# Second pass of graph attention on one core: the Newton step of a tile moved between the scans and the next tile's rows, ScalarE's norms ahead of its squares

## What is computed

```python
alpha = e_exp / (denom[dst] + 1e-16)          # a softmax over the edges of a dst node, 8 heads
msg = h[src] * alpha[:, :, None]
out = segment_sum(msg, dst)                   # 256 features
x1 = layernorm(x + relu(out + bias))          # eps 1e-5, over the 256 features
```

## Time and profile before

| what | value |
|---|---|
| median of 3 runs | 1858.53 us (1857.64 to 1864.1) |
| profiled execution, its own time | 1859.5 us |
| its span in the profile | 1857.8 us |
| TensorE / VectorE busy | 62% / 68% of the span |
| ScalarE / GpSimd busy | 54% / 54% |
| second pass of attention | from about 540 to 716 us of the span |
| first convolution | from 716.7 us |

### The profile page before, as it was taken

The page is one execution under the profiler, slowest core; times in us unless marked ns, Lnnn a source line. Parts: engine busy times, 40 slices in busy tenths (PEclk is TensorE's granted clock), DMA queues, the critical chain, the costliest instruction groups (busy, mean ns, idle before and its releaser), DMA issues.

```text
span 1857.8 us, 17164 instructions
## 1 busy us (share of the span) xinstructions
PE 1146.6 (62%) x3863; PEld 584.9 (31%) x3863; DVE 1264.9 (68%) x3084; ACT 997.7 (54%) x2650; POOL 998.6 (54%) x1032
## 2 busy tenths in 40 slices
PE   0148888850039972999995999897999891000000
PEld 0023333310014431555552455454444451000000
DVE  8847777769889980555552556464666697778887
ACT  4736877765446772344442465454555454555654
POOL 1057766677777667777763777406444077720000
PEclk9999999975555555999997999998999996555555
DMA  8367899977865653788883566857765288999998
GB/s 360 116 212 233 278 350 375 356 243 230 254 235 174 208 186 112 221 261 266 260 241 113 136 176 178 169 147 128 150 138 128 75 278 327 372 351 350 351 342 315
DMA packets 177393, 436.13 MB, mean 235 GB/s; under 512 B 28804, under 2 KB 108810, under 8 KB 157324
## 3 DMA queue, kind: packets, MB, share of 16 engines
q1 hardware_dynamic: 109020, 229.52, 35.8%
q0 software_dynamic: 44800, 100.49, 21.6%
q10 hardware_dynamic: 23472, 105.03, 15.6%
HBM read 257.16 MB, written 182.32 MB: 237 GB/s over the span
## 4 chain that ended last, share of the span: by engine, by line
PE 30%; DVE 27%; DMA 17%; POOL 11%; issue 8%; ACT 7%; SPq 1%; ACTq 0%; DVEq 0%; POOLq 0%
DMA arena<-x 13%; PE ps L1247 10%; PE ps L1260 10%; POOL arena L1218 4%; DVE arena L1510 3%; DVE arena L1493 3%; PE ps L1237 3%; DVE stat L782 3%; ACT arena L821 3%; POOL arena L1199 3%; POOL slot L679 3%; PE ps L1424 2%; DVE arena L779 2%; DVE arena L1043 2%; DVE big L1052 2%
## 5 line engine op out<-in xcount | busy, mean ns | idle before, releaser
L1332 DVE TENSOR_TENSOR_SCAN arena<-arena,ps 128x512 f32<-128x512 f32 x150 | 190.9, 1276 | 267.2 <-PE ps L1247 240.1
L836 POOL DMA_INDIRECT arena<-x,idx x200 | 189.8, 949 | 173.2 <-DVE idx L603 90.9
L1218 POOL DMA_INDIRECT arena<-agg,slot x200 | 189.1, 945 | 173.5 <-PE ps L1237 75.4
L1247 PE MATMUL ps<-arena 128*128 128x512 f32 x600 | 277.0, 605 | 7.0 <-DVE arena L1332 7.0
L1260 PE MATMUL ps<-arena 128*128 128x512 f32 x600 | 275.6, 603 | 8.9 <-ACT arena L1302 8.9
L1524 ACT ACTIVATE arena<-arena 128x256 f32<-128x256 f32 x391 | 156.6, 402 | 140.0 <-DVE arena L1493 140.0
L1199 POOL DMA_INDIRECT arena<-x,idx x200 | 189.1, 946 | 62.0 <-issue 59.1
L821 ACT ACTIVATE arena<-arena,shift,inv 128x256 f32<-128x256 f32 (+1 forms) x311 | 156.1, 588 | 51.4 <-DVE shift L813 34.6
L1336 DVE TENSOR_TENSOR ps<-arena,ps 128x512 f32<-128x512 f32 x150 | 103.8, 695 | 105.9 <-PE ps L1260 105.9
L1461 POOL DMA_INDIRECT x<-big,idx x100 | 123.9, 1239 | 88.4 <-DVE big L1451 53.7
L1302 ACT ACTIVATE arena<-big,bn_shift,bn_scale 128x512 f32<-128x512 f32 x100 | 75.9, 806 | 165.6 <-PE ps L1260 153.8
(11 more groups left out here) (213 smaller groups left out, 2234.0 us busy)
## 6 DMA issues: line engine op xcount, KB each, us to landing
arena<-x SPq DMA_DIRECT2D x39, 1280.0 KB, 7.8
out<-arena SPq DMA_DIRECT2D x39, 1280.0 KB, 5.4
arena<-x ACTq DMA_DIRECT2D x31, 1280.0 KB, 10.2
x<-arena ACTq DMA_DIRECT2D x31, 1280.0 KB, 6.5
agg<-arena SPq DMA_DIRECT2D x50, 512.0 KB, 4.2
arena<-not_same SPq DMA_DIRECT2D x75, 256.0 KB
arena<-last_of SPq DMA_DIRECT2D x75, 256.0 KB
x_dst<-arena SPq DMA_DIRECT2D x25, 512.0 KB, 4.9
```

Of the source, the lines that this page charges most:

```text
L836: pl.indirect_dma_start(rows_in[:, par, a, g, :], None, x[:, :], bass.IndirectOffsetOnAxis(ap=idx[:, k, t * G + g:t * G + g + 1], axis=0)) ...
L1218: pl.indirect_dma_start(conv_in[:, b, 1, g, :], None, agg_dram[l - 1][:, :], bass.IndirectOffsetOnAxis(ap=slot[:, t * G + g:t * G + g + 1] ...
L1247: m = pe.matmul(far_bank[j], thp[:, l, 0, k, j * P:(j + 1) * P], far_t[:, par, k, :], start=(k == 0), stop=(k == 1))
L1332: v.tensor_tensor_scan(runmax[:, par, j, :], mask[:, tl % 2, :], far_bank[j], initial, ALU.add, ALU.max).then_inc(s_conv_scan, 1)
```

## The change

Two lists of stages are changed; no instruction is added, removed or altered. VectorE runs `finish` with lag 2 in place of 3, and between `sums` and `rows`. ScalarE runs `normed` with lag 1 in place of 2, and ahead of `stds`. All other engines' lists are the same.

```diff
@@ -1071,7 +1071,7 @@
                 v.wait_ge(s_x1_newton, 4 * t + 4)
                 v.scalar_tensor_tensor(inv1[:, par, :], d, 1.5, near, ALU.add, ALU.mult).then_inc(s_x1_shift, 1)
                 v.scalar_tensor_tensor(shift1[:, par, :], d, 1.5, off, ALU.add, ALU.mult).then_inc(s_x1_shift, 1)
-            in_steps([(3, finish), (0, sums), (1, rows)], NS)
+            in_steps([(0, sums), (2, finish), (1, rows)], NS)
 
         def msg_pe(pe):
             pe.wait_ge(s_h_kept, 2 * NS)
@@ -1117,7 +1117,7 @@
                     o = x1_big[:, t, n, :]
                     m = a.activation(o, o, ACT.Identity, scale=inv1[:, par, n:n + 1], bias=shift1[:, par, n:n + 1])
                 m.then_inc(s_x1_normed, 1)
-            in_steps([(0, stds), (2, normed)], NS)
+            in_steps([(1, normed), (0, stds)], NS)
 
         def x1_pool(pl):
             all_stored(pl)
```

## The result

The changed kernel takes 1849.76 us (median of 6 runs, 1848.18 to 1854.47), the kernel before 1860.68 in the same comparison (1857.64 to 1864.1). The ratio is 0.9939, 95% interval 0.9923 to 0.9956: 0.6% faster, by 10.9 us. Forecast were 1848.5, a range of 1845.0 to 1853.5 and a gain of 10.0.

What follows compares the result with a forecast made beforehand. The late norm of tile 21 was taken to bound the pass; 1.8 us of VectorE's pace and earlier last norms made 10.0 us, so 1859.5 - 10.0 = 1849.5, forecast as a median of 1848.5 us, range 1845.0 to 1853.5.

Steps and rivals of the forecast that it cites:

- What bounds the pass: End of the pass: the late norm of tile 21, behind the squares of tile 23, sets when the last scatters end.
- (2) VectorE's pace: VectorE in the pass: mean pace 6.02 us a tile, tile 24's multiply 1.8 us earlier, between 0 and 3.1.
- Rival B: VectorE's mean is held by the whole scatter it meets, 0.25 us a tile on average; 1852.3 us, chance 0.04.
- (3) No waits in the loop: Loop of the pass: neither Newton step nor TensorE's alphas cause waits; cost 0, bounds of 0 to 0.3 us a tile.
- ScalarE's ring: Norm, squares, root and VectorE's Newton step, 5.3 us together, fit into a tile of 6.0; margin 0.6.
- (4) The last tiles: End of the pass, from tile 24's multiply: last scatter at 704.3 against 714.33, 10.0 us earlier.
- GpSimd is free then: Last tile: GpSimd is done with tile 23 by 700.3, so tile 24's scatters start at 700.4, behind its norm.
- the sign that I had announced: GpSimd in the pass: waits for norms (L1118) some 9 times, starting about tile 16, not 18 times.
- the sum's 163.6 us: From the pass's first multiply to the forecast last scatter: 704.3 - 540.7.
- (5) What follows: Stages after the pass: all move 10.0 us earlier with the first gathers, none of it taken back.
- C without gain: The last scatter is held by something other than norms, GpSimd ends near 714 as before; 1858.5 us, chance 0.05.
- D: Norm, squares, root and Newton step become the loop and VectorE waits; slower, from 1868 us, chance 0.03.

Runs made afterwards that it cites:

- the change under the other conditions: The same change profiled again on chips where the kernel before takes about 2234 us; ratio 0.9920 to that kernel, first multiply to first gather 166.0 us.
- the longer ring: The change plus three unused ScalarE instructions per tile between norm and next squares; ratio 0.9962 to the kernel before, first multiply to first gather 171.5 us.

## Why the prediction was right, and where not

- **What bounds the pass** (the norm of tile 21 behind the squares of tile 23): right. ScalarE's list alone, which ends just this, takes 6.7 us off the end of the pass (32.4 to 25.7), beside 3.5 of pace.
- **(2) VectorE's pace**: tile 24's multiply was forecast at 682.5 and came at 682.47. That is partly luck: the pass began 0.9 us later, and the 21 tiles from the multiply of tile 3 (556.89) took 125.6 us, 5.98 each, in place of 6.02. The free pace is 5.93 (586.62 to 592.55 below), not 5.96, and 4 means were held noticeably (three by scatters, one by a lookup ahead of them), not 5. They took up to 0.45, not 0.37.

```profile
586.62 0.17 DVE L1055 TENSOR_SCALAR mean<-sum 128x4 f32<-128x4 f32 x1
...
592.00 0.99 POOL L1127 DMA_INDIRECT x<-big,idx  x1 [0.30 <-issue]
...
592.55 0.43 DVE L1055 TENSOR_SCALAR mean<-sum 128x4 f32<-128x4 f32 x1
```

  The mean at 592.55, 0.55 into a scatter, again ends with it (592.98 and 592.99). Rival B, by which any mean inside a scatter would be held, is out: every mean of the change 0.26 to 0.51 into one took 0.17 us. Two sums of the section were off. A mean that is 0.25 longer would make 6.21 of 5.96, while the tile takes 6.15, so a held mean costs the tile some 0.19. And a mean that starts 0.68 in and is held to 0.98 loses 0.13, not 0.07. In the change under the other conditions, where GpSimd goes in step with VectorE throughout, nothing settles at 0.68 and 6.03 either: the means start in turn some 0.60 and 0.79 into the fourth scatter, take 0.38 and 0.19 and end with it, and the tiles take 6.13 and 5.93. The few that start at 0.27, 0.43 or 0.83 take 0.17. From tile 3's multiply to tile 24's that makes 126.4 us, 6.02 a tile, just the pace forecast. The Trainium skill (SBUF — State Buffer, "SBUF: two separate sides") has the lock for the whole instruction of whichever starts first; the traces agree with its end, not with its beginning.
- **(3) No waits in the loop**: right. The margin of ScalarE's ring is 0.7 us by the longer ring, where 0.6 was worked out. What the section missed is the wait of `finish(t)` for the norm of tile t-2. It costs nothing in the change because both lists were changed together, and 18.5 to 19 us if only VectorE's is.
- **(4) The last tiles**: the times forecast for VectorE and ScalarE held to 0.2 us (Newton steps at 691.34 and 696.61, the last norm over at 699.54 in place of 699.7). But the last scatter came at 705.6, not 704.3. The step that failed is "GpSimd is free then": it took the start of the scatters, 570.57, from one execution as given. It came 7.2 us later, and this sets the end at 577.75 + 127.84. So the sign that I had announced, some 9 waits from tile 16 on, did not come either. Where GpSimd is early, the sum's 163.6 us after the first multiply was met (163.7).
- **(5) What follows**: -8.8 at the first gather and -10.3 in the span. That the size agrees with the forecast of 10.0 in the span is luck, two small misses against each other: 1.3 less at the last scatter and 1.6 more behind it.
- **Rivals C and D**: C without gain is out, as the last scatter came 8.7 us earlier on the same step of 1.29, with the same 2.3 us to the gather. D is out for the change: no Newton step waited before the last two tiles.

## What to carry to other kernels

When two engines pass a tile to and fro with lags, write down for each step what it waits for on the other engine's queue and what stands there ahead of it: the order of "finish the old tile" and "begin the new one" on the engine downstream was worth 10 us here (6.7 for the shorter way of the last tiles, 3.5 because the means met the scatters at another place), the same reordering upstream only 0.4, and alone it cost 19. A reordering of two engines is one change, and its halves must be tried as such. And look at the consumer's own queue before crediting a producer: in the first profile of the change GpSimd's own queue was the limit, 1.4 us behind the norms.

## What was not expected of the hardware

- The small multiply with one input in SBUF is held by a scatter on GpSimd only if it starts well inside: 0.26 to 0.49 into the 0.98 us it takes 0.17, at 0.53 to 0.64 it takes 0.31 to 0.45 and ends with the scatter. At 0.51 into one (610.58 and 676.42 in the change) it still took 0.17. So the hold begins between 0.51 and 0.53 us into the scatter. From 0.75 on little of the scatter is left, and it takes 0.17 to 0.23. A lookup on GpSimd holds it as a scatter does (0.40 long at 561.12 in the kernel before, 0.54 into the lookup). With a second input in SBUF it was never held, in 25 tiles of each of two kernels, at up to 0.66 into a scatter.
- Three ScalarE instructions of 128x256 with neither a scale or shift per row nor a sum took 1.01 us, 0.34 each; four with scale and shift per row took 2.06, and four squares with a sum 0.49 apart each.
